# First attention layer: three PSUM banks for the maxima, one for all full-array groups, and the key copy on ScalarE

## The reference, cut to what matters

```python
x = x + _layernorm(_L0_attn_ref(_layernorm(x), w_qkv, b_qkv, w_o, b_o))

qkv = jnp.einsum('bld,ed->ble', x, w_qkv) + b_qkv          # in _L0_attn_ref
q, k, v = jnp.split(qkv, 3, axis=-1)                       # 16 heads of 8
attn = jax.nn.softmax(jnp.einsum('blhc,bmhc->bhlm', q, k) * SCALE, axis=-1)
heads = jnp.einsum('bhlm,bmhc->blhc', attn, v).reshape(b, l, d)
return jnp.einsum('bld,ed->ble', heads, w_o) + b_o + x
```

## Time and profile before

| what | before |
|---|---|
| median of 3 runs | 680.53 us (680.42 to 681.06) |
| profiled execution | 686.72 us, its span 685.0 us |
| TensorE matmul busy | 564.5 us (82%) |
| VectorE busy | 463.5 us (68%) |
| ScalarE busy | 360.5 us (53%) |
| GpSimd busy | 327.0 us (48%) |
| granted clock of TensorE, mean | 0.881 of full |

### The profile page before, as it was taken

The page is one execution under the profiler, slowest core; times in us unless marked ns, Lnnn a source line. Parts: engine busy times, 40 slices in busy tenths (PEclk is TensorE's granted clock), DMA queues, the critical chain, the costliest instruction groups (busy, mean ns, idle before and its releaser), DMA issues. The chain is left out here.

```text
span 685.0 us, 16070 instructions
## 1 busy us (share of the span) xinstructions
PE 564.5 (82%) x5228; PEld 420.9 (61%) x5228; DVE 463.5 (68%) x1301; ACT 360.5 (53%) x957; POOL 327.0 (48%) x543
## 2 busy tenths in 40 slices
PE   3899999999999999999993689886987408999930
PEld 2565566666666666666552577776876408999920
DVE  1455778777877777777742588888687633788870
ACT  0214545555554555565451498886774004676750
POOL 5230244332245655541213636775888750257776
PEclk9657999999999999999976799999886557999975
DMA  4200523010000000000011000000000122234333
GB/s 128 41 2 2 156 64 49 8 20 17 18 18 18 17 11 10 18 18 18 18 28 36 31 2 1 2 2 1 15 23 24 39 79 66 49 47 63 41 31 31
DMA packets 38099, 21.62 MB, mean 32 GB/s; under 512 B 13433, under 2 KB 36353, under 8 KB 38018
## 3 DMA queue, kind: packets, MB, share of 16 engines
q1 hardware_dynamic: 18544, 10.65, 7.0%
q0 software_dynamic: 6640, 4.92, 5.1%
q10 hardware_dynamic: 12834, 5.04, 3.0%
HBM read 10.11 MB, written 8.12 MB: 27 GB/s over the span
## 5 line engine op out<-in xcount | busy, mean ns | idle before, releaser
L352 DVE TENSOR_REDUCE nmax<-psA 128x2 f32<-128x512 f32 x256 | 165.4, 688 | 81.2 <-PE psA L214 77.2
L509 ACT ACTIVATE pr<-psB 128x512 f32<-128x512 f32 x250 | 135.8, 595 | 153.1 <-PE psB L231 148.7
L214 PE MATMUL psA<-km,qp 24*128 24x256 f32 x768 | 146.4, 425 | 13.0 <-DVE nmax L352 6.5
L214 PEld LDWEIGHTS psA<-km,qp 24*128 24x128 f32 x768 | 97.7, 196 | 47.8 <-DVE nmax L352 30.7
L231 PE MATMUL psB<-q,km 26*128 26x256 f32 (+1 forms) x752 | 110.7, 411 | 0.0
L597 POOL TENSOR_TENSOR km<-kraw,rows_of 128x768 f32<-128x768 f32 x16 | 23.5, 1468 | 172.1 <-DVEq L331 166.4
L1613 POOL DMA_INDIRECT out<-wz,ys x39 | 63.4, 1625 | 54.8 <-ACT wz L1568 46.0
L245 PE MATMUL psO<-pr,v 128*32 128x256 f32 x1024 | 71.1, 397 | 0.1
L231 PEld LDWEIGHTS psB<-q,km 26*128 26x128 f32 (+1 forms) x752 | 69.5, 190 | 0.2
L1176 ACT ACTIVATE prob<-psS,nbias 128x128 f32<-128x128 f32 x128 | 45.6, 382 | 11.7 <-DVE nbias L995 11.7
L245 PEld LDWEIGHTS psO<-pr,v 128*32 128x32 f32 x1024 | 27.2, 111 | 33.8 <-issue 23.1
(11 more groups left out here) (198 smaller groups left out, 1179.4 us busy)
## 6 DMA issues: line engine op xcount, KB each, us to landing
q<-mT SPq DMA_DIRECT2D x256, 1.0 KB
ys<-y_sorted SPq DMA_DIRECT2D x39, 72.0 KB, 1.9
e_w<-W ACTq DMA_DIRECT2D x1, 2048.0 KB
e_w<-W ACTq DMA_DIRECT2D x4, 512.0 KB
xs<-x_all SPq DMA_DIRECT2D x16, 128.0 KB
out<-x_all SPq DMA_DIRECT2D x15, 128.0 KB, 3.7
x_all<-x SPq DMA_DIRECT2D x1, 1536.0 KB, 9.0
out<-wz,ys POOLq DMA_INDIRECT x39
```

What stands on the lines that cost most here:

```text
L214: last = T.matmul(psA[:, n % 2, c * L1:(c + 1) * L1], query_part(b, h, depth, c), keys(b, h, depth, slice(0, L1)), start=True, stop=True)
L352: V.tensor_reduce(nmax[:, b % 2, hf, :, at], psA[:, n % 2, :].rearrange("p (c m) -> p c m", c=2), AX.X, ALU.max, negate=True).then_inc(S[" ...
L509: A.activation(pr[:, h % PRING, :, :].rearrange("p c l -> p (c l)"), bank_of(b, h), ACT.Exp, scale=SCALE1).then_inc(S["b_free"], 1)
```

## The change

Three things are done at once in the first layer.

1. `psA` has three banks instead of two, so that head n waits for head n-3 instead of head n-2.
2. `misc` has one bank instead of two. Every full-array group now waits until the one before it has been taken out of PSUM. The groups of a pass move: `prep_x` from round 0 to round 1 (behind `attend`), both halves of the queries to round 2, both halves of the keys to round 4, `project` from round 7 to round 6, `prep_v` from round 2 to round 7 (behind `attend`). Round 0 has none.
3. The keys are taken out by ScalarE in two instructions, ahead of the exponentials of round 5, instead of by VectorE in one in round 6. The reordered queries `qp` are made from `q` in SBUF, in round 6, instead of from PSUM. VectorE takes `residual` in round 7 of the same pass instead of round 0 of the next, and `residual_stats` and `stats_x` move to rounds 0 and 1.

```diff
-        psA = pb("psA", [P, 2, 512])
+        psA = pb("psA", [P, 3, 512])
-        misc = [pb(f"misc{k}", [P, 512]) for k in range(2)]
+        misc = pb("misc", [P, 512])
...
-            for what, b in (("xT", i + 2), ("v", i + 1), ("q", i + 2), ("k", i + 2), ("out", i - 1)):
+            for what, b in (("xT", i + 2), ("q", i + 2), ("k", i + 2), ("out", i - 1), ("v", i + 1)):
...
             def begin(*name):
-                bank, before = turns[name]
-                pe.wait_ge(S[f"free{bank}"], before)
-                return bank
+                pe.wait_ge(S["free"], turns[name])
...
-                pe.wait_ge(S["a_free"], count(16 * b + n - 1))
+                pe.wait_ge(S["a_free"], count(16 * b + n - 2))
...
-                    last = T.matmul(psA[:, n % 2, c * L1:(c + 1) * L1],
+                    last = T.matmul(psA[:, (16 * b + n) % 3, c * L1:(c + 1) * L1],
...
# TensorE, iteration(i)
-                    if g == 0 and fits(i, 2):
-                        prep_x(i + 2)
                     if g == 1 and done:
                         attend(i - 1, 3)
-                    if g == 2 and i >= 1 and next_:
+                    if g == 1 and fits(i, 2):
+                        prep_x(i + 2)
+                    if g in (2, 4) and fits(i, 2):
+                        prep_qk(i + 2, g // 2 - 1, 0)
+                        prep_qk(i + 2, g // 2 - 1, 1)
+                    if g == 6 and done:
+                        project(i - 1)
+                    if g == 7 and i >= 1 and next_:
                         prep_v(i + 1)
-                    if g in (3, 4) and fits(i, 2):
-                        prep_qk(i + 2, 0, g - 3)
-                    if g == 6 and fits(i, 2):
-                        prep_qk(i + 2, 1, 0)
-                        prep_qk(i + 2, 1, 1)
-                    if g == 7 and done:
-                        project(i - 1)
# VectorE, iteration(i); keys_in is gone, also from the prologue
                     if g == 0 and fits(i, -2):
-                        residual(i - 2)
-                    if g == 1 and fits(i, -2):
                         residual_stats(i - 2)
+                    if g == 1 and fits(i, EARLY):
+                        stats_x(i + EARLY)
...
-                    if g == 4 and fits(i, EARLY):
-                        stats_x(i + EARLY)
...
-                    if g == 6 and fits(i, 2):
-                        keys_in(i + 2)
+                    if g == 7 and done:
+                        residual(i - 1)
# ScalarE
+            def keys_in(b):
+                ready("k", b)
+                act.wait_ge(S["b_full"], count(16 * (b - SLOTS + 1)))
+                act.wait_ge(S["km_ok"], count(b - SLOTS + 1))
+                for t in range(2):
+                    A.activation(kraw[:, b % SLOTS, t, :], misc[:, t * L1:(t + 1) * L1], ACT.Identity,
+                                 bias=b_cols[:, 2 + t:3 + t]).then_inc(S["k_ok"], 1)
+                act.wait_ge(S["k_ok"], 2 * b + 2)
+                act.sem_inc(S["free"])
...
+                    if g == 5 and fits(i, 2):
+                        keys_in(i + 2)
                     if here:
                         exponentials(i, 2 * g)
                         exponentials(i, 2 * g + 1)
-                    if g == 0 and fits(i, 2):
+                    if g == 0 and i >= 2 and here:
+                        values_in(i)
+                    if g == 1 and fits(i, 2):
                         turned_x(i + 2)
-                    if g == 2 and i >= 1 and next_:
-                        values_in(i + 1)
-                    if g == 4 and fits(i, 2):
+                    if g == 3 and fits(i, 2):
                         queries_in(i + 2)
+                    if g == 6 and fits(i, 2):
+                        queries_in_parts(i + 2)
...
# ScalarE, prologue
             for b in range(2):
                 turned_x(b)
                 queries_in(b)
+                keys_in(b)
+                queries_in_parts(b)
```

More of the change, by code:

```diff
@@ L161, in _ @@
             for k in range(4):
-                last = T.transpose(misc[bank][:, k * P:(k + 1) * P], w_nat[:, k, :], ident[:, :])
-            last.then_inc(S[f"full{bank}"], 1)
-            bank = begin("bias")
+                last = T.transpose(misc[:, k * P:(k + 1) * P], w_nat[:, k, :], ident[:, :])
+            last.then_inc(S["full"], 1)
+            begin("bias")
             pe.wait_ge(S["brow0"], 4)
@@ L168, in _ @@
                 for t in range(2):
-                    last = T.matmul(misc[bank][:, 2 * k + t:2 * k + t + 1], brow[0:1, k, t, :], one[:, :],
+                    last = T.matmul(misc[:, 2 * k + t:2 * k + t + 1], brow[0:1, k, t, :], one[:, :],
                                     start=True, stop=True)
-            last = T.matmul(misc[bank][:, 4:5], bv_row[0:1, :], one[:, :],
-                            start=True, stop=True)
-            last.then_inc(S[f"full{bank}"], 1)
+            last = T.matmul(misc[:, 4:5], bv_row[0:1, :], one[:, :], start=True, stop=True)
@@ L175, in prep_x @@
+            last.then_inc(S["full"], 1)
             def prep_x(b):
-                bank = begin("xT", b)
+                begin("xT", b)
                 pe.wait_ge(S["xn_ok"], b + 1)
                 for c in range(2):
-                    last = T.transpose(misc[bank][:, c * P:(c + 1) * P], xn[:, b % 2, c, :], ident[:, :])
-                last.then_inc(S[f"full{bank}"], 1)
+                    last = T.transpose(misc[:, c * P:(c + 1) * P], xn[:, b % 2, c, :], ident[:, :])
+                last.then_inc(S["full"], 1)
@@ L182, in prep_qk @@
             def prep_qk(b, k, t):
                 if t == 0:
-                    made, n = turns[("xT", b)]
-                    pe.wait_ge(S[f"free{made}"], n + 1)
+                    pe.wait_ge(S["free"], turns[("xT", b)] + 1)
                     begin("qk"[k], b)
-                bank, _ = turns[("qk"[k], b)]
-                made = T.matmul(misc[bank][:, t * L1:(t + 1) * L1], wqk[:, k, t, :], xnT[:, b % 2, :], start=True,
+                made = T.matmul(misc[:, t * L1:(t + 1) * L1], wqk[:, k, t, :], xnT[:, b % 2, :], start=True,
@@ L189, in prep_qk, with token_major @@
                                 stop=True)
                 if t == 1:
-                    made.then_inc(S[f"full{bank}"], 1)
-            def token_major(lhs, k, bank):
+                    made.then_inc(S["full"], 1)
+            def token_major(lhs, k):
                 for c in range(2):
-                    last = T.matmul(misc[bank][:, c * P:(c + 1) * P], lhs[:, c * P:(c + 1) * P], wvo[:, k, :],
+                    last = T.matmul(misc[:, c * P:(c + 1) * P], lhs[:, c * P:(c + 1) * P], wvo[:, k, :],
@@ L197, in token_major @@
                                     start=True, stop=True)
-                last.then_inc(S[f"full{bank}"], 1)
+                last.then_inc(S["full"], 1)
             def prep_v(b):
-                bank = begin("v", b)
-                token_major(xnT[:, b % 2, :], 0, bank)
+                begin("v", b)
+                token_major(xnT[:, b % 2, :], 0)
             def scores_for_max(b, n):
@@ L251, in project @@
                 pe.wait_ge(S["onT_ok"], b + 1)
-                bank = begin("out", b)
-                token_major(onT, 1, bank)
+                begin("out", b)
+                token_major(onT, 1)
             def iteration(i):
@@ L580, in norm_x @@
                 if b >= 2:
-                    bank, before = turns[("xT", b - 2)]
-                    pool.wait_ge(S[f"full{bank}"], before + 1)
+                    pool.wait_ge(S["full"], turns[("xT", b - 2)] + 1)
                 for c in range(2):
```

88 lines of the change are left out of this document (35 added, 53 removed).

## The result

The changed kernel takes 679.58 us (median of 20 runs) against 681.53 us of the kernel before (20 runs as well). Without five runs of the changed kernel that lie over 1.5% above its fastest, its mean is 678.0 us against 682.9, a ratio of 0.9928 (interval 0.9900 to 0.9957): 4.9 us or 0.7% faster. With them it is 3.5 us, and the two medians are 1.95 us apart. Forecast were 11.4 us. Its runs lie far apart, from 671.9 to 686.1 us, and with them the mean granted clock, 0.903 in the fastest and 0.883 in the slowest. The profiled execution has a span of 677.5 us against 685.0.

A forecast was written before the change was run, and what follows sets the result against it. TensorE was taken to set the pace, partly by standing still; gains of 4.4 (prologue, pass 0), 11.0 (passes 1 to 13) and 5.0 (pass 14), less 9 for clock falls, made 11.4 us: 669 us, range 659 to 681.

The forecast's parts named there:

- passes 1 to 13 at full clock: First layer's passes: each 18.95 us, 0.85 less than before, 11.0 us in all.
- pass 14: Rounds back to back, then at half clock: 17.65 instead of 23.1 us if the clock holds; 5 us taken.
- a dip at a lean place: From round 7's `attend` into the next round 1: little TensorE work halves the clock in 2 to 3 of 13 passes, 9 us.
- VectorE loses 0.68 of work and gains none: VectorE's load per pass: the moved evacuations take 0.68 us from it and add nothing.
- the cover given for the moved keys: Round 5: ScalarE's key copies (0.84 us) fit its 8.7 idle us and end before round 5's exponentials are ready.
- The sum of a pass: 19.79 us less 2.42 of waits and 0.5 of mode changes, plus 1.0, 1.0 and 0.1 of new waits: 18.95.
- Every wait that was said to go: Second heads of rounds 1, 3, 5, 7 (2.08 us) and first heads after x's transposes and a query half (0.16, 0.18).
- the three that were said to come: Round 1 on round 0's first reduction, 1.0 us; `prep_v` on `residual`, 1.0; the keys on the queries' evacuation, 0.1.
- rivals 3 and 4: Third: `misc`'s single bank binds every group, about 680 us, chance 0.09. Fourth: exponentials limit, third bank useless, 676, 0.05.
- Rival 1: The clock holds in every pass: 660 us, chance 0.25.
- rival 2: The clock falls in more than half of the passes: eight falls would give 688 us, slower; chance 0.11.
- From the profile to the median: Profiled execution forecast at 675.3 us; the median taken to lie 6.2 us below it, at 669.

The follow-up runs named there:

- e1: Changed kernel with GpSimd's products and sums for the experts' bias moved ahead of `add_attention`; 666.4 us, ratio 0.973 to the kernel before.
- e5: Changed kernel with five more pairs of GpSimd products and sums on a scratch tile in passes 2 to 6; 702.9 us, ratio 1.029.
- e10: Kernel before with only GpSimd's bias work moved ahead of `add_attention`; 685.2 us, ratio 1.002.
- e9: Changed kernel with `prep_v` moved to round 0 of the next pass, bias work left where it was; 645.4 us, ratio 0.944.
- e2: Changed kernel with VectorE's residual at the head of round 7, ahead of the maxima and the turn; 655.8 us, ratio 0.958.
- e7: e1 with each pass's keys taken out by VectorE at the head of its round 5 instead of by ScalarE; 663.9 us, ratio 0.967.
- e3: Changed kernel with only two of the three banks of `psA` used, and the wait of two banks; 715.2 us, ratio 1.035.
- e8: e4 with only two of the three banks of `psA` used; 673.0 us, ratio 0.986.
- e11: e4 with ScalarE's loads of the experts' weights started in passes 3 to 7 instead of 1 to 5; 645.0 us, ratio 0.943.
- e4: Changed kernel with the bias work moved as in e1 and `prep_v` moved to round 0 of the next pass; 640.0 us, ratio 0.935.
- e6: e4 again unchanged, a single run to look at its clock; 637.5 us.

## Why the prediction was wrong

The direction was right and the amount was not: 11.4 us forecast, 7.5 between the two profiles, 4.9 between the means; the range of 659 to 681 us held the time near its upper end. Between the two profiles, in us:

| step | forecast | measured |
|---|---|---|
| prologue and pass 0 (pass 1 begins at 66.2 instead of 71.55) | -4.4 | -5.3 |
| passes 1 to 13 at full clock (18.39 instead of 19.79) | -11.0 | -18.2 |
| pass 14 (17.5 instead of 23.1) | -5.0 | -5.6 |
| three collisions with their dips (91.25 - 73.56) | 0 | +17.7 |
| a dip at a lean place (pass 20.02 long) | +9 | +1.6 |
| pass 1, late rows of maxima (20.20 long) | 0 | +1.8 |
| the rest | 0 | +0.5 |

That the range held is luck in part: the passes at full clock gained 7.2 us more than forecast, and that hid as much of the 17.7 us.

**The step that failed** is "VectorE loses 0.68 of work and gains none", with the cover given for the moved keys. The keys reach GpSimd 4.8 us earlier in a pass, what stands behind their spreading in its queue moves with them, and there, in three passes, is a sum that blocks the normalisation. The prediction followed VectorE, ScalarE and SyncE and never asked what the moved keys start on GpSimd. The rows for it were there: in the kernel before the same sum began right behind the spreading of the keys. The three collisions and their dips cost 17.7 us, a term that the prediction put at nothing. e1, e5 and e10 show this cause; e9 and e2 show that it needs the wait ahead of `prep_v` to be so dear: the same block of 2.2 us costs 2.5 us with nothing behind the residual (e9) and 3.3 with the reductions and the turn no longer between it and the residual (e2), instead of 5.9.

**The clock.** The amount taken for it, 9 us, was half of the 19.3 us that clock and collisions took together, and for another reason. Lean places alone took one dip in each of three profiles (changed kernel, e1, e7), not two to three. That the dip of pass 14 would go was right: the clock held there at full until pass 15. The price was mis-sized too: a dip of 10.24 us without a collision cost 4.8 us in a full pass (e1) and 4.4 in pass 14 (e7), not 3.5. In it TensorE has a matmul in its pipe for 10.20 of 10.20 us, so little makes up for the lower clock.

**The sum of a pass** was 0.56 us too high, mostly in three terms: the change of mode from x's transposes to a round takes 0.17 and not 0.33 (109.18), from the values 0.12 (102.36 and 104.17 are `attend` and the values, 104.69 their end, 104.81 the round), and the wait for the residual costs 0.81 and not 1.0. Every wait that was said to go went (e3 and e8 give 1.7 and 1.8 us a pass for the third bank, its largest part), and the three that were said to come came, at their places. So rivals 3 and 4 are out: in a plain pass no group but the values waited for the single bank by more than 0.1 us, and the exponentials did not take over. Rival 1, the clock that holds in every pass, did not happen in the changed kernel; nor did rival 2, whose eight dips came only when e5 forced them with eight collisions.

**From the profile to the median** the prediction took off 6.2 us, the distance between the two in the kernel before, and so came from 675.3 to 669. That step failed as well: the profiled execution of the changed kernel took 679.28 us, and its median is 679.58. The 20 runs of the kernel before fall into two groups, eleven from 679.9 to 681.6 us and nine from 684.0 to 686.8; its profile is one of the upper. What tells the groups apart no trace here shows.

**SyncE's maxima** were given ten microseconds. No pass but pass 1 waits for them, where the experts' weights keep the DMA engines busy (0.79; e11).

Open is why of two equal stretches (e1, 254.99 and 273.38) one trips the clock. How much of the 5.9 us is the block and how much the clock can be estimated in two ways: the dip of e1, 4.8 us, leaves 1.1 for the block; the longer stand-still, 3.09 less 1.23, leaves 4.0 for the clock. No kernel here had the full block without a dip and with the wait behind it, so neither is shown.

## What to carry to other kernels

When a step moves to an earlier time, follow what it releases on every queue, also on engines that have much idle time: what runs behind it there moves too, and may meet an instruction that it never met before. A short VectorE operation with two inputs in SBUF in front of a wait of TensorE is a bad neighbour for a long GpSimd operation that reads SBUF: here 0.29 us became 2.20. And a last buffer is best kept free of a reader that stands behind two microseconds of other work: putting one group between two rounds, where its bank was long free, gave 1.46 us of 18.39 per pass and took the lean place away with it (e4).

## What the runs showed of the hardware

Unexpected were the price and the regularity of the clock's dips. Every stand-still of TensorE of about 2.6 to 3.1 us (gaps ahead of a weight load, in passes 1 to 13) was followed by half clock, eleven times in e5 and the changed kernel, for 10.24 us nine times and 6.8 us twice. Three of 1.65 us in e2 were followed by it once. One of 1.23 us did it once in each of three profiles of some thirteen passes (the changed kernel, e1, e7), and where none was longer than 0.41 us it never came between 90 and 309 us (e4, e6). A normalisation that takes 0.29 us alone and began 0.3 to 0.5 us after GpSimd's sum took as long as the rest of that sum and 0.15 us more, twenty times out of twenty (the changed kernel, e2, e3, e5, e9).
